# A sixth key step of each group summed by GpSimd for the softmax denominators of a 16-head cross attention, TensorE left with one

## The chip, the cores and the metric

One core of one Trainium2 chip runs the kernel. The metric is device time in microseconds (us) of one launch; less is better. Time before: 4722.19 us, the median of 3 runs (4709.07 to 4722.22).

## The reference, cut to what matters

The program runs four layers, each an attention block and a feed-forward block with a residual, on x (8 batches of 256 tokens, 128 wide) and a context (8 batches of 1601 tokens, 64 wide). The change is in the second attention of layer 1 only: 16 heads of 32, queries from x, keys and values from the normalized context.

```
H, D, C1, C2, S, M, B, W = (16, 32, 128, 64, 256, 64, 2, 4)
q = jnp.einsum('bsc,hcd->bhsd', xn, wq)
k = jnp.einsum('btc,hcd->bhtd', yn, wk)
v = jnp.einsum('btc,hcd->bhtd', yn, wv)
a = jax.nn.softmax(jnp.einsum('bhsd,bhtd->bhst', q, k) * D ** (-0.5), axis=-1)
o = jnp.einsum('bhst,bhtd->bhsd', a, v)
o = o.transpose(0, 2, 1, 3).reshape(x.shape[0], x.shape[1], H * D)
x_out = x + o @ li1_w + li1_b
```

The sum over the keys that softmax divides by (the denominator) is what the change is about.

## The kernel before, in words

The function `wide_cross` computes this attention. The work is cut into 32 groups (`NG`): 8 batches by 4 groups of 4 heads, a head on 32 partitions. The 1601 keys of a group are 13 tiles of up to 128 keys, taken two at a time in 7 key steps w = 0 to 6 (`NW`); the last step has one tile of 65 keys.

The order of the work is written out by hand: `wide_plan` repeats one list, `period`, for every n, and each engine walks through the same plan and does those steps that are its own, strictly in that order. An entry ("scores", 0, w) belongs to group n, ("max", 1, i) to group n+1, ("sums", -1) to group n-1. The steps are:

- "max": TensorE multiplies queries by keys (line 1800) into a ring of three PSUM banks, and VectorE takes the row maxima from there (line 1904). The ring is used by one such step at a time: the matmuls of the next wait until VectorE has read it. The eleventh step ends with VectorE's small reduction to the negated maximum `negm` (line 1909).
- "cut": after the eleventh "max" step of a group GpSimd splits `negm` into two bf16 pieces, `max_pieces` (a cast, line 1960, and a subtraction, line 1962). It stands in GpSimd's queue behind the additions of the group before.
- "neg": TensorE transposes the pieces (line 1810) into the ring, VectorE copies them out as `max_rows` (line 1917).
- "scores": TensorE puts the negated maxima (line 1773) and queries by keys (line 1778) for one key step into the four score banks; ScalarE takes the exponential into one of four buffers `probs` (line 1879, two instructions; line 1884 for the last step). `NPR` is 4, so the exponential of a key step waits for whoever still reads the buffer of four key steps earlier.
- "weigh": TensorE multiplies `probs` by the values (line 1821).
- the denominators: GpSimd copies the `probs` of w = 0 to `sums` (line 1949) and adds those of w = 1 to `NADD`-1 to it (line 1952), each as soon as ScalarE has written it. TensorE then multiplies a matrix of ones by `sums` (line 1829) and, for the key steps from `NADD` on, by `probs` itself (line 1834).
- "take": VectorE inverts the denominators (line 1925) and scales the output (line 1927). The next group's "weigh" of w = 0 waits for it.
- "kproj", "vproj", "qproj": projections of keys (line 1788, two groups ahead), values (line 1760, one ahead) and, for n = 2, 6, 10, ..., queries (line 1749); "out" (line 1844) for n = 4, 8, ... is the output projection.

The end of the period, the seam to the next group, reads:

```
("scores", 0, 6), ("max", 1, 9), ("kproj", 2),
("max", 1, 10), ("weigh", 0, 5), ("max", 2, 0), ("vproj", 1), ("neg", 1), ("weigh", 0, 6), ("max", 2, 1)]
```

and its start `("scores", 0, 0), ("max", 1, 2), ("sums", -1), ("qproj", 2), ("take", -1), ("max", 1, 3), ("scores", 0, 1)`. The waits that the prediction speaks of are these, in TensorE's "neg" and "sums" and in GpSimd's part:

```
pe.wait_ge(cut, 2 * n + 2)
pe.wait_ge(added, NADD * n + NADD)
for w in range(NADD, NW):
if kind == "scores" and step[2] < NADD:
    pool.wait_ge(added, NADD * n + w)
elif kind == "max" and step[2] == 10:
    pool.wait_ge(placed, n + 1)
```

Of the kernel before, what the change touches and what calls it, by code (L numbers as in the profile page):

```python
# [1635 lines left out]


NW = 7
NADD = 5
NPR = 4  # L1640


# [35 lines left out]
def wide_cross(nc, k, scale, ctx_t, xt, wq, wk, wv, w1, b1, x, xo):  # L1678
    plan, slot, ring = wide_plan()
    with ExitStack() as ctx:  # L1680
# [29 lines left out]
        def wait_drained(eng, step):  # L1710
            eng.wait_ge(s_free, slot[step] + 1)
# [15 lines left out]
        def rows(j):  # L1727
            return slice(32 * j, 32 * j + 32)
# [13 lines left out]
        def _(pe):  # L1742
            for step in plan:
# [80 lines left out]
                elif kind == "sums":  # L1824
                    n = step[1]
                    pe.wait_ge(added, NADD * n + NADD)
                    for i in range(2):
                        for j in range(4):
                            pe.matmul(lbank[rows(j), :], ones_f[:], acc[:, n % 2, j, i, :], start=(i == 0), stop=False)
                    for w in range(NADD, NW):  # L1830
                        wait_drained(pe, ("scores", n, w))
# [17 lines left out]
        def _(act):  # L1849
            for step in plan:  # L1850
# [15 lines left out]
                elif kind == "scores":  # L1866
                    n, w = step[1], step[2]
                    u = NW * n + w
                    if u >= NPR:
                        m, before = (u - NPR) // NW, (u - NPR) % NW  # L1870
                        act.wait_ge(pv_done, u - NPR + 1)
                        if before < NADD:
                            act.wait_ge(added, NADD * m + before + 1)
                        else:
# [61 lines left out]
        def _(pool):  # L1936
# [4 lines left out]
            for step in plan:  # L1941
                kind = step[0]
                if kind == "scores" and step[2] < NADD:
                    n, w = step[1], step[2]
# [5 lines left out]
                    else:  # L1950
                        pool.wait_ge(added, NADD * n + w)
                        pool.tensor_tensor(o, o, p, ALU.add).then_inc(added, 1)  # L1952
# [633 lines left out]
```

## Time and profile before

| | |
|---|---|
| median of 3 runs | 4722.19 us |
| the profiled execution | 4737.31 us |
| its span | 4735.6 us |
| TensorE busy | 3735.6 us (79%) |
| VectorE busy | 2568.1 us (54%) |
| ScalarE busy | 1959.9 us (41%) |
| GpSimd busy | 935.6 us (20%) |
| the stage of this attention | about 2117 to 3262 us of the span |

The profile comes from one execution on the chip. PE is TensorE's matmuls, PEld its weight loads, DVE is VectorE, ACT ScalarE, POOL GpSimd. Busy time is the time in which an engine had an instruction running; it says nothing of which engine the others wait for. PEclk is the clock that TensorE was granted, 1.00 being 2.4 GHz and 0.50 being 1.2 GHz.

### The profile page before, as it was taken

Reading aid. Unit: us, or ns where it says so; the run is one execution under the profiler, and the core shown is the slowest. Engines: PE = TensorE matmul, PEld = TensorE weight load, DVE = VectorE, ACT = ScalarE, POOL = GpSimd, SP = SyncE. Lnnn points to the kernel's source line nnn. Section 1 sums busy time; section 2 is a strip of 40 time slices with the busy share of each in tenths; the row PEclk is TensorE's granted clock in tenths of the full one; section 3 lists DMA queues with packets and bytes.
Section 4 is the critical chain, followed back from the end, with each engine's and each line's share of the span. In section 5 each row is a group of like instructions: output and inputs, shape, how many; then the busy total and the mean of one; then the engine's idle time right before and its main releaser. Section 6 shows DMA issues by size and latency. Waiting matters only on the chain. (4 is left out here: it accounts for less than half of the span.)

```text
span 4735.6 us, 83741 instructions
## 1 busy us (share of the span) xinstructions
PE 3735.6 (79%) x32681; PEld 1978.3 (42%) x32681; DVE 2568.1 (54%) x4933; ACT 1959.9 (41%) x2627; POOL 935.6 (20%) x546
## 2 busy tenths in 40 slices
PE   6887699999559999628999999997587669999932
PEld 4665233332336666413444444444355323333312
DVE  3434587877254455244555555552242557788856
ACT  2333376777123333223444444443121136677721
POOL 0000111110000000023656565563000011111000
PEclk9998699999579999858999999998787768999966
DMA  0000312110000000030000000000021031111000
GB/s 15 0 0 19 64 29 45 31 36 10 2 12 0 0 0 0 7 78 1 9 8 9 9 8 6 4 2 8 10 53 35 21 63 28 37 37 36 13 5 9
DMA packets 68487, 89.57 MB, mean 19 GB/s; under 512 B 37808, under 2 KB 48718, under 8 KB 68174
## 3 DMA queue, kind: packets, MB, share of 16 engines
q1 hardware_dynamic: 59416, 75.78, 7.2%
q10 hardware_dynamic: 8758, 9.41, 0.9%
q8 instruction: 220, 3.60, 0.3%
q14 instruction: 93, 0.76, 0.1%
HBM read 34.53 MB, written 4.33 MB: 8 GB/s over the span
## 5 line engine op out<-in xcount | busy, mean ns | idle before, releaser
L1592 DVE TENSOR_REDUCE mx<-ps 128x2 f32<-128x802 f32 (+1 forms) x1372 | 1028.0, 778 | 295.0 <-PE ps L1458 271.5
L1526 ACT ACTIVATE probs<-ps 128x1024 f32<-128x1024 f32 (+1 forms) x832 | 832.9, 1024 | 256.0 <-PE ps L1444 247.1
L1904 DVE TENSOR_REDUCE mx<-ps 128x3 f32<-128x1203 f32 (+1 forms) x352 | 483.2, 1373 | 476.2 <-PE ps L1800 476.2
L1952 POOL TENSOR_TENSOR sums<-sums,probs 128x2048 f32<-128x2048 f32 x128 | 579.0, 4523 | 142.5 <-ACT probs L1879 128.8
L1458 PE MATMUL ps<-kt,qs 48*128 48x401 bf16 x2048 | 472.8, 356 | 112.1 <-DVE mx L1592 75.3
L1476 PE MATMUL ps<-probs,v_cur 128*9 128x256 f32 x6656 | 530.7, 392 | 0.4 <-ACT probs L1526 0.4
L1879 ACT ACTIVATE probs<-ps 128x1024 f32<-128x1024 f32 x384 | 372.1, 1021 | 358.2 <-PE ps L1778 358.1
L1800 PE MATMUL ps<-kt,qt 32*128 32x401 f32 x2048 | 338.3, 554 | 47.1 <-DVE mx L1904 41.5
L1444 PE MATMUL ps<-qs,kt 50*128 50x256 bf16 (+1 forms) x3328 | 347.6, 282 | 1.8 <-ACT probs L1526 1.4
L462 PE MATMUL ps<-kk,q 128*128 128x256 f32 (+1 forms) x1024 | 277.2, 390 | 25.2 <-ACT kk L541 20.8
L1458 PEld LDWEIGHTS ps<-kt,qs 48*128 48x128 bf16 x2048 | 134.9, 95 | 328.7 <-DVE mx L1592 251.4
L539 ACT ACTIVATE q<-ps,qb 32x256 f32<-32x256 f32 (+1 forms) x256 | 119.5, 467 | 348.1 <-PE ps L455 344.0
L1778 PE MATMUL ps<-qt,kt 32*128 32x256 f32 (+1 forms) x3328 | 251.1, 375 | 0.0
L1444 PEld LDWEIGHTS ps<-qs,kt 50*128 50x128 bf16 (+1 forms) x3328 | 111.3, 97 | 327.8 <-issue 153.5
L547 ACT ACTIVATE probs<-ps 128x384 f32<-128x384 f32 (+1 forms) x256 | 137.9, 542 | 259.4 <-PE ps L483 135.2
L1821 PE MATMUL ps<-probs,v_cur 128*32 128x256 f32 (+1 forms) x3328 | 227.0, 387 | 12.9 <-issue 12.7
L1633 POOL CAST max_pieces<-negm 128x8 bf16<-128x8 f32 x64 | 12.1, 189 | 1120.9 <-DVE negm L1597 1120.9
L462 PEld LDWEIGHTS ps<-kk,q 128*128 128x128 f32 x1024 | 184.0, 202 | 68.4 <-ACT kk L541 32.1
L1800 PEld LDWEIGHTS ps<-kt,qt 32*128 32x128 f32 x2048 | 110.6, 186 | 200.5 <-DVE mx L1904 119.0
L1778 PEld LDWEIGHTS ps<-qt,kt 32*128 32x128 f32 (+1 forms) x3328 | 188.0, 180 | 12.0
L568 DVE TENSOR_REDUCE mpad<-ps 128x2 f32<-128x512 f32 x128 | 88.7, 693 | 185.5 <-PE ps L462 183.5
L168 PE MATMUL ps<-ident,xn 128*128 128x128 f32 x160 | 41.4, 430 | 179.4 <-DVE xn L154 179.4
(382 smaller groups left out, 5243.7 us busy)
## 6 DMA issues: line engine op xcount, KB each, us to landing
kt<-k SPq DMA_DIRECT2D x776, 50.0 KB
ctx_s<-in_ctx_t SPq DMA_DIRECT2D x16, 400.2 KB, 4.8
ctx_s<-ctx_norm_t SPq DMA_DIRECT2D x16, 400.2 KB, 5.4
qs<-q ACTq DMA_DIRECT2D x24, 192.0 KB
ctx_norm_t<-ctx_norm_t SPq DMA_DIRECT2D x8, 400.2 KB, 3.7
ctx_a<-in_ctx_t SPq DMA_DIRECT2D x8, 400.2 KB, 4.3
ctx_b<-in_ctx_t SPq DMA_DIRECT2D x8, 400.2 KB
ctx_tok<-in_ctx SPq DMA_DIRECT2D x8, 384.0 KB
```

The lines of the kernel that those rows point to most:

```text
L462: ins = pe.matmul(ring(step)[:, S * qt:S * qt + nk], q1[:, g, j, P * qt:P * qt + P], kk[:, g, 0:nk], start=True, stop=True)
L1444: ins = pe.matmul(pair[0:m, j, S * (jj // 2):S * (jj // 2) + S], kt[rows, b % 2, g, P * t:P * t + m], qs[rows, g, S * b:S * b + S], start= ...
L1458: ins = pe.matmul(bank(step, i)[:, 0:CH], qs[rows, g, tok:tok + P], kt[rows, b % 2, g, lo:lo + CH], start=True, stop=True)
L1476: ins = pe.matmul(obank[32 * jj:32 * jj + 9, :], v[0:m, b % 2, t, 9 * h:9 * h + 9], pr[0:m, u % 3, at:at + S], start=(t == 0), stop=(t == ...
L1526: act.activation(pr[0:m, u % 3, :], pair[0:m].rearrange("p a n -> p (a n)"), ACT.Exp, scale=scale).then_inc(s_free, 1)
L1592: dve.tensor_reduce(mx[:, n % 2, i0:i0 + count], src, AX_X, ALU.max).then_inc(freed(step), 1)
L1778: ins = pe.matmul(sbanks[0:m, j, S * i:S * i + S], kt[rows(j), n % 4, P * t:P * t + m], qt[rows(j), b % 2, a, :], start=False, stop=(i == ...
L1800: ins = pe.matmul(rbanks[:, i - 3 * i0, 0:CH], qt[rows(j), b % 2, a, q:q + P], kt[rows(j), n % 4, lo:lo + CH], start=True, stop=True)
L1821: ins = pe.matmul(obank[rows(j), :], v[0:m, n % 2, t, rows(j)], pr[0:m, (NW * n + w) % NPR, j, i, :], start=(t == 0), stop=(t == KT - 1))
L1879: ins = act.activation(pr[:, u % NPR, 2 * f:2 * f + 2, :, :].rearrange("p j i n -> p (j i n)"), sbanks[:, 2 * f:2 * f + 2, :].rearrange("p ...
L1904: dve.tensor_reduce(mx[:, n % 2, 3 * i0:3 * i0 + count], rbanks[:, 0:count, 0:CH], AX_X, ALU.max).then_inc(ring_free, 1)
L1952: pool.tensor_tensor(o, o, p, ALU.add).then_inc(added, 1)
```

## The change

The constant `NADD` goes from 5 to 6. No other line changes.

```diff
 NW = 7
-NADD = 5
+NADD = 6
 NPR = 4
```

On GpSimd, the seam between two groups: `sums` are the running denominators, `max_pieces` the split maxima of the next group. Before:

```order
226 L1960 CAST max_pieces<-negm 128x8
227 L1962 TENSOR_TENSOR max_pieces<-negm,max_pieces 128x8
228 L1949 COPY sums<-probs 128x2048
229 L1952 TENSOR_TENSOR sums<-sums,probs 128x2048 x4
230 L1960 CAST max_pieces<-negm 128x8
231 L1962 TENSOR_TENSOR max_pieces<-negm,max_pieces 128x8
```

And with the change:

```order
226 L1960 CAST max_pieces<-negm 128x8
227 L1962 TENSOR_TENSOR max_pieces<-negm,max_pieces 128x8
228 L1949 COPY sums<-probs 128x2048
229 L1952 TENSOR_TENSOR sums<-sums,probs 128x2048 x5
230 L1960 CAST max_pieces<-negm 128x8
231 L1962 TENSOR_TENSOR max_pieces<-negm,max_pieces 128x8
```

A fifth addition stands ahead of the cast and the subtraction of every group.

On TensorE, the start of a group: the scores of w = 0, a "max" step, the denominators of the group before (lines 1829 and 1834), the next "max" step and the scores of w = 1:

```order
@@ -2046,5 +2046,5 @@
 L1800 MATMUL ps<-kt,qt 128x401 x3
 L1829 MATMUL ps<-sums,ones_f 32x256 x8
-L1834 MATMUL ps<-probs,ones_f 32x256 x12
+L1834 MATMUL ps<-probs,ones_f 32x256 x4
 L1800 MATMUL ps<-kt,qt 128x401 x3
 L1773 MATMUL ps<-max_rows,ones_b 128x512 x4
```

Eight of twelve matmuls on `probs` are gone; the order of the rest is the same. The instructions of VectorE and ScalarE are the same ones in the same order.

## Rows read from the trace of the kernel before

**Rows 1.** Busy time of each engine over the stage of this attention.

```profile
core 0: us, PE busy (x) PEld busy (x) DVE busy (x) ACT busy (x) POOL busy (x), PEclk, DMA share, GB/s
2117.00:3262.00 1145.00, 1024.57 (x12236) 535.73 (x12236) 569.28 (x486) 515.87 (x553) 654.55 (x227) 0.98 0.03 7
```

**Rows 2.** Groups of GpSimd's instructions by line, in the stage.

```profile
L1952 POOL TENSOR_TENSOR sums<-sums,probs 128x2048 f32<-128x2048 f32 x128 | 579.0, 4523 | 142.5 <-ACT probs L1879 128.8
```

**Rows 3.** Timeline, GpSimd, four groups on end: start, duration, engine, line, [idle before].

```profile
2587.25 18.55 POOL L1952 TENSOR_TENSOR sums<-sums,probs 128x2048 f32<-128x2048 f32 x4 [3.55 <-ACT probs L1879]
2610.03 0.22 POOL L1960 CAST max_pieces<-negm 128x8 bf16<-128x8 f32 x1 [4.24 <-DVE negm L1909]
...
2623.20 18.51 POOL L1952 TENSOR_TENSOR sums<-sums,probs 128x2048 f32<-128x2048 f32 x4 [3.56 <-ACT probs L1879]
2643.21 0.22 POOL L1960 CAST max_pieces<-negm 128x8 bf16<-128x8 f32 x1 [1.50 <-DVE negm L1909]
2643.51 0.23 POOL L1962 TENSOR_TENSOR max_pieces<-negm,max_pieces 128x8 bf16<-128x8 f32 x1
...
2658.79 18.54 POOL L1952 TENSOR_TENSOR sums<-sums,probs 128x2048 f32<-128x2048 f32 x4 [5.97 <-ACT probs L1879]
2678.37 0.22 POOL L1960 CAST max_pieces<-negm 128x8 bf16<-128x8 f32 x1 [1.04 <-DVE negm L1909]
...
2691.54 18.53 POOL L1952 TENSOR_TENSOR sums<-sums,probs 128x2048 f32<-128x2048 f32 x4 [3.55 <-ACT probs L1879]
2711.53 0.22 POOL L1960 CAST max_pieces<-negm 128x8 bf16<-128x8 f32 x1 [1.46 <-DVE negm L1909]
```

**Rows 4.** Timeline, the seam after the group whose additions began at 2623.20.

```profile
2643.93 1.82 PE L1760 MATMUL ps<-wv,ctx_s 64*128 64x128 f32 x26
2645.68 0.29 PE L1810 MATMUL ps<-identb,max_pieces 128*128 128x128 bf16 x2
...
2646.47 0.95 PE L1800 MATMUL ps<-kt,qt 32*128 32x401 f32 x6
2647.51 0.10 PEld L1773 LDWEIGHTS ps<-max_rows,ones_b 2*128 2x128 bf16 x4 [0.74 <-ACT v_cur L1865]
2647.54 1.41 DVE L1904 TENSOR_REDUCE mx<-ps 128x3 f32<-128x1203 f32 x1 [1.18 <-PE ps L1800]
2649.01 0.95 PE L1800 MATMUL ps<-kt,qt 32*128 32x401 f32 x6 [0.24 <-DVE mx L1904]
```

**Rows 5.** Timeline, the denominators at the start of a group.

```profile
2616.90 1.41 DVE L1904 TENSOR_REDUCE mx<-ps 128x3 f32<-128x1203 f32 x1 [1.13 <-PE ps L1800]
2617.60 1.48 PE L1834 MATMUL ps<-probs,ones_f 128*32 128x256 f32 x24
2619.01 0.61 PE L1800 MATMUL ps<-kt,qt 32*128 32x401 f32 x3
2621.18 1.94 ACT L1879 ACTIVATE probs<-ps 128x1024 f32<-128x1024 f32 x2 [3.49 <-PE ps L1778]
```

**Rows 6.** The instructions of line 1834: duration of one pass in ns, min/median/max.

```profile
L1834 PE MATMUL ps<-probs,ones_f x768: 377/379/634, 2205.1 to 3259.9; 128*32 128x256 f32 x128, 65*32 65x256 f32 x64
```

**Rows 7.** Timeline, the last group's denominators.

```profile
3256.34 1.93 PE L1829 MATMUL ps<-sums,ones_f 128*32 128x256 f32 x16 [2.23 <-POOL sums L1952]
3258.04 2.28 PE L1834 MATMUL ps<-probs,ones_f 128*32 128x256 f32 x24
```

**Rows 8.** Timeline of TensorE near the stage's end.

```profile
3223.79 0.94 PE L1800 MATMUL ps<-kt,qt 32*128 32x401 f32 x4 [1.61 <-DVE mx L1904]
...
3225.73 3.35 PE L1760 MATMUL ps<-wv,ctx_s 64*128 64x128 f32 x26
...
3244.68 0.39 PE L1773 MATMUL ps<-max_rows,ones_b 2*128 2x512 bf16 x4 [1.15 <-ACT probs L1879]
```

**Rows 9.** Windows there, columns as in rows 1.

```profile
3224.00:3228.00 4.00, 4.00 (x40) 2.78 (x40) 1.20 (x2) 0.00 (x0) 1.73 (x3) 0.69 0.00 0
3244.00:3248.00 4.00, 2.26 (x36) 1.22 (x36) 0.00 (x0) 2.53 (x3) 3.86 (x2) 1.00 0.00 0
```

## The prediction

> **What bounds the kernel now.** I first took the busy times over the stage [rows 1]. It lasts 1145 us. TensorE is busy 1025 of them, GpSimd 655, VectorE 569, ScalarE 516. Read alone, that says: TensorE is full, GpSimd has 490 us to spare, so work should go from the one to the other. Busy time does not say who waits for whom at the place where the work is put, so I went on to the timelines.
>
> GpSimd's timeline [rows 3] shows one pattern per group. Four additions run end to end, 18.5 us in all, from the moment the exponential of w = 1 is done; call that moment S. GpSimd is never idle between them. A short wait for `negm` follows, and then the cast. That wait is the real slack of GpSimd here: 1.50, 1.04 and 1.46 us in three groups of four, 4.24 us in the one that holds the output projection. The idle time that makes up the rest of the 490 us lies elsewhere, ahead of the copy and between the copy and the first addition, where the new addition can't go, since w = 5 is not computed yet.
>
> The seam [rows 4] shows who needs the cast. TensorE runs the values' projection, the transposes of the pieces right at its end, then a "max" step at 2646.47, whose read by VectorE ends at 2648.95, and the next "max" step at 2649.01, 0.06 us later. The ring is handed over without slack: a transpose that comes late makes both steps late, then the denominators behind them, the scores of w = 1, and the next S.
>
> **The change, part by part.** Every group repeats; I work per group and multiply.
>
> *The addition.* One addition takes 4.52 us [rows 2]; four take 18.53, so they start every (18.53 - 4.52) / 3 = 4.67 us [rows 3]. Five end at S + 4 x 4.67 + 4.52 = S + 23.2. The w = 5 data should be there: GpSimd ran through w = 1 to 4 without idle time, so each of them was ready before it came to it, and w = 5 has until S + 18.6, 4.67 us longer than w = 4, whereas its two exponentials take 1.94 us [rows 5]. The cast can begin at S + 23.3.
>
> *How late that is.* Before, the casts began at S + 22.78, 20.01, 19.58 and 19.99 for the four kinds of group [rows 3]. So they move by 0.5, 3.3, 3.7 and 3.3 us.
>
> *What hides a part of it.* From the cast's start to the transposes it was 2645.68 - 2643.21 = 2.47 us [rows 3, 4]. What has to lie there is the cast and the subtraction, 0.53 us in all (2643.21 to 2643.74), and the step from GpSimd to TensorE. The hand-overs in the rows take 0.06 us, for instance VectorE's read that ends 2648.95 and TensorE's step at 2649.01 [rows 4]; I take that for GpSimd too, whose own hand-over to TensorE at the stage's end [rows 7] is of the same kind. So 2.47 - 0.59 = 1.9 us of lateness cost nothing; the values' projection covers them. What is left is 0, 1.4, 1.8 and 1.4 us. If the cover did not exist it would be the whole 3.3 to 3.7; if the later wait for ScalarE's values copy (0.74 us of TensorE's idle time, at 2647.51 [rows 4]) hid more, it would be 0.7 to 1.1. I take 1.4 and 1.8, since the "max" steps of the ring don't wait for that copy and they are the longer way.
>
> Of the 31 seams 24 are of the late kinds: 8 of 1.8 (a query projection in the group) and 16 of 1.4. 8 x 1.8 + 16 x 1.4 = 36.8 us.
>
> *The eight matmuls taken away.* Twelve matmuls are 24 passes and take 1.48 us, of which the last pass's own 0.38 us [rows 6] is not shortened: (1.48 - 0.38) / 23 x 16 = 0.77 us less [rows 5]. The "max" step behind them begins 2619.01 and would begin 18.24, but VectorE frees the ring at 2618.31 [rows 5]; so 0.64 us are won, and 0.77 where the query projection stands between. This is on the path: ScalarE waits 3.49 us for the scores of w = 1 behind it [rows 5]. Bounds: nothing, if something else held w = 1, and 0.77 in all. 30 groups have it inside the stage: 23 x 0.64 + 7 x 0.77 = 20.1 us won.
>
> *The stage's end.* After the last group TensorE already waits 2.23 us for GpSimd [rows 7]; one more addition is 4.67 us on the path, and the eight matmuls less, at the half clock there, give back (2.28 - 0.63) / 23 x 16 = 1.15 [rows 6, 7]. Net 3.5 us.
>
> Sum so far: 36.8 + 3.5 - 20.1 = +20 us.
>
> *The clock.* The steady stage has no pause of TensorE as long as the new ones. Near its end it has two kinds [rows 8, 9]: pauses of 1.15 us in every key step leave the granted clock at 1.00 (3244 to 3248), and one of 1.61 us, at 3222.18 to 3223.79, is followed by 0.69 in 3224 to 3228. The clock fell to its lower level, 1.2 GHz, and the values' projection took 3.35 us there, against 1.82 at 2.4 GHz [rows 4, 8]. The new pauses, between the projection and the transposes, are as long as the lateness: 1.4 us lies between the pause that was harmless and the one that was not, 1.8 us a little above both. The 24 seams all have one. The longest cost that I see for a fall is those 1.5 us; the least is nothing, when the slow stretch lies where TensorE waits for ScalarE or GpSimd anyway. Behind the seam TensorE's steps are on the path, so I take 1.2. With half of the seams it is 12 x 1.2 = +14 us; with none 0, with all and 1.5 each +36.
>
> In the Trainium skill, the page "TensorE: Matmul & The Clock Gate", section "Why this matters for your kernels", warns only of pauses longer than any that this change makes. By that rule no seam would lose the clock and the sum would stop at +20. The 1.61 us pause in this trace speaks against relying on it.
>
> **Sum: +20 + 14 = +34 us.** Against its own execution that is 4737.31 + 34 = 4771 us. That execution is 15 us (0.3%) above the median of the runs shown; against the median it is 4722.2 + 34 = 4756 us, +0.7%. A difference under 0.3%, 14 us, can't be told from none.
>
> **The rivals.**
>
> *The clock never falls* (chance 0.22). For it: pauses of 1.15 us never cost it. Against: the 1.61. Time: +20 us, 4742.
>
> *It falls at every seam, at full price* (0.10). +20 + 36 = +56, 4778. For it: the one pause of 1.61 us was followed by a fall. Against: 16 of the new pauses are shorter than that one.
>
> *The values copy covers more* (0.12). If the scores of w = 0 and not the ring led to the next S, the lateness would shrink by the 0.74 us of that wait at each seam: 36.8 - 24 x 0.74 = 19.0, and 19.0 + 3.5 - 20.1 = +2: 4724, no change. Against it: VectorE's hand-over of the ring at 2649.01 with no slack.
>
> *Faster* (0.06). One mechanism: the seam can absorb all of the late cast. It would take a path from the seam to S that has 1.4 to 1.8 us more slack than the rows show, for instance if TensorE took the shortened denominators and the "max" steps before the transposes; the plan has them behind. Then only the eight matmuls and the end count: 3.5 - 20.1 = -17 us, 4705. It decides at a lateness of 0.7 us per seam (20.1 - 3.5, over 24); I work out twice that.
>
> *The fifth case, mine: some seams lose the clock* (0.50).
>
> That the change would not do what it says is excluded: the order of instructions has the fifth addition ahead of each cast and four matmuls in the place of twelve.
>
> **How the numbers follow.** The likeliest case is +34: 4756. From +14 (the first rival, less the small noise of a median) to +60 the clock cases lie, 0.82 together; leaving out the two lower rivals would be 0.18. So the range is 4736 to 4782. Slower by over 0.3%: the case itself 0.50, all seams 0.10, and most of the 0.22, together 0.79. Within 0.3%: 0.12 and the rest of the 0.22, 0.15. Faster: 0.06.
>
> **What would show it.** GpSimd: five additions in 23.2 us, then the cast with hardly any idle time ahead of it, in all groups. TensorE: a wait for GpSimd's `max_pieces` of 1.4 or 1.8 us ahead of line 1810 in three groups of four, none in the fourth. Line 1834: 8 passes per group instead of 24, about 0.7 us. Four groups together grow by 1.9 us where the clock holds: lateness 1.4 + 1.8 + 1.4 = 4.6, less 3 x 0.64 + 0.77 = 2.7. The granted clock: stretches at 0.50 behind seams in a steady part that had none. The prediction is wrong if the wait ahead of line 1810 is under 0.7 us, if S does not follow the transposes one for one, or if the granted clock stays at 1.00 (then about 4742) or falls behind all seams (about 4778).

## The result and the profile after

| | before | after |
|---|---|---|
| median | 4719.67 us (4 runs) | 4751.32 us (4 runs, 4749.49 to 4759.3) |
| profiled execution | 4737.31 us | 4759.3 us |
| span | 4735.6 us | 4757.5 us |

The ratio is 1.0075, 95% interval 1.0055 to 1.0094: the kernel is 0.75% slower. 4756 us were forecast.

The stage of the cross attention, which answers to [rows 1], from the view of windows (columns as there):

```profile
2117.00:3285.00 1168.00, 1017.29 (x11700) 536.25 (x11700) 567.63 (x485) 516.00 (x553) 791.10 (x258) 0.95 0.03 8
2200.00:3200.00 1000.00, 891.60 (x10420) 476.23 (x10416) 506.68 (x436) 454.60 (x488) 704.06 (x228) 0.97 0.03 6
```

The steady 1000 us of the kernel before, to compare with the second of these rows:

```profile
2200.00:3200.00 1000.00, 916.92 (x11144) 482.26 (x11142) 518.38 (x444) 468.40 (x503) 592.53 (x203) 1.00 0.03 6
```

TensorE has fewer instructions and GpSimd more, as wanted. But the granted clock, which was 1.00 in this part before, is now 0.97.

GpSimd's timeline for two groups, which answers to [rows 3]:

```profile
2780.74 23.19 POOL L1952 TENSOR_TENSOR sums<-sums,probs 128x2048 f32<-128x2048 f32 x5 [2.92 <-ACT probs L1879]
2803.89 0.21 POOL L1960 CAST max_pieces<-negm 128x8 bf16<-128x8 f32 x1
...
2816.72 23.19 POOL L1952 TENSOR_TENSOR sums<-sums,probs 128x2048 f32<-128x2048 f32 x5 [5.37 <-ACT probs L1879]
2839.85 0.22 POOL L1960 CAST max_pieces<-negm 128x8 bf16<-128x8 f32 x1
2840.15 0.23 POOL L1962 TENSOR_TENSOR max_pieces<-negm,max_pieces 128x8 bf16<-128x8 f32 x1
```

The rows of the cast have no bracket any more: GpSimd does not wait for the maxima, the maxima wait for GpSimd. In the late kinds of group the cast begins 23.12 to 23.15 us after S (S is the start of the first addition), where it was 19.4 to 20.3 before.

The seam behind the second of these groups, as the timeline shows it, answers to [rows 4]:

```profile
2837.02 1.82 PE L1760 MATMUL ps<-wv,ctx_s 64*128 64x128 f32 x26
...
2840.44 0.29 PE L1810 MATMUL ps<-identb,max_pieces 128*128 128x128 bf16 x2 [1.60 <-POOL max_pieces L1962]
...
2842.50 1.93 PE L1778 MATMUL ps<-qt,kt 32*128 32x256 f32 x14
2843.88 1.73 PE L1800 MATMUL ps<-kt,qt 32*128 32x401 f32 x6
```

TensorE stands 1.60 us before the transposes, and GpSimd's subtraction is what ends the wait. The scores and the "max" step behind it are then slow: six passes of line 1800 take 1.73 us and not the 0.95 of [rows 4]. That is the lower clock, in a window of the same place (columns as above):

```profile
2841.00:2846.00 5.00, 5.00 (x49) 3.08 (x45) 1.81 (x3) 1.41 (x2) 0.00 (x0) 0.66 0.56 131
```

How often TensorE waits there is in the view of line 1810, what ended the idle time ahead of it (us, times). Each seam counts twice, for the matmul and for its weight load, so these are 24 seams. TensorE's own pause is 1.1 to 1.8 us in 23 of them and 3.21 us in the last:

```profile
  POOL max_pieces L1962: 79.9, 48
```

And the end of the stage, in the timeline, answers to [rows 7]:

```profile
3291.80 1.94 PE L1829 MATMUL ps<-sums,ones_f 128*32 128x256 f32 x16 [6.88 <-POOL sums L1952]
3293.51 1.08 PE L1834 MATMUL ps<-probs,ones_f 65*32 65x256 f32 x8
```

The wait for GpSimd's last addition is 6.88 us, 4.65 longer.

**A measure for the experiments.** The stage can be cut out of each trace: from the first S to the last S (31 group lengths), and from the last S to the end of VectorE's last read of the output projection. In the trace before the additions start at 2177.52 and 3237.76, and that read ends at 3268.44. After:

```profile
2181.24 4.53 POOL L1952 TENSOR_TENSOR sums<-sums,probs 128x2048 f32<-128x2048 f32 x1 [4.06 <-ACT probs L1879]
...
3268.59 4.52 POOL L1952 TENSOR_TENSOR sums<-sums,probs 128x2048 f32<-128x2048 f32 x1 [2.03 <-ACT probs L1879]
```

So the groups took 1060.24 us before and 1087.35 after (+27.1), the end 30.7 and 34.4 (+3.7). What lies behind the stage is the same code in every kernel here, yet took 1467 us in the trace before and 1449 to 1459 in the others. That is why single spans say less than the stage, and why the whole launches are compared by medians. Each stage time comes from one execution of its kernel; how well such times repeat shows where two kernels do the same: 29 of the 31 groups of e1_cut_first below are as long as those of e3_matmuls_only within 0.01 us.

### The profile page after: what moved, and what is told of

Same layout as the page of the kernel before. It is cut to its first block and busy times, and to the rows that moved or that the text cites. A ratio compares the mean times of both kernels' runs of the same rounds, so it can differ in the third digit from the quotient of the medians.

```text
span 4757.5 us, 82781 instructions
## 1 busy us (share of the span) xinstructions
PE 3719.5 (78%) x32169; PEld 1974.9 (42%) x32169; DVE 2567.6 (54%) x4933; ACT 1960.9 (41%) x2627; POOL 1079.3 (23%) x578
## 5 line engine op out<-in xcount | busy, mean ns | idle before, releaser
L1952 POOL TENSOR_TENSOR sums<-sums,probs 128x2048 f32<-128x2048 f32 x160 | 723.7, 4523 | 131.0 <-ACT probs L1879 112.3
L1800 PE MATMUL ps<-kt,qt 32*128 32x401 f32 x2048 | 353.5, 572 | 49.4 <-DVE mx L1904 42.2
L1778 PE MATMUL ps<-qt,kt 32*128 32x256 f32 (+1 forms) x3328 | 277.3, 394 | 0.0
L1778 PEld LDWEIGHTS ps<-qt,kt 32*128 32x128 f32 (+1 forms) x3328 | 204.0, 190 | 14.1
```

The source lines that it names most:

```text
L1778: ins = pe.matmul(sbanks[0:m, j, S * i:S * i + S], kt[rows(j), n % 4, P * t:P * t + m], qt[rows(j), b % 2, a, :], start=False, stop=(i == ...
L1800: ins = pe.matmul(rbanks[:, i - 3 * i0, 0:CH], qt[rows(j), b % 2, a, q:q + P], kt[rows(j), n % 4, lo:lo + CH], start=True, stop=True)
```

## The experiments

| run | median us | before beside it | ratio (95% interval) | first to last S | end | falls of the clock between them |
|---|---|---|---|---|---|---|
| kernel before | | | | 1060.2 | 30.7 | 1 |
| kernel after | 4751.3 | 4719.7 | 1.0075 (1.0055 to 1.0094) | 1087.3 | 34.4 | 15 |
| e1_cut_first | 4708.3 | 4719.4 | 0.9983 (0.9966 to 1.0) | 1032.1 | 34.4 | 0 |
| e2_add_only | 4772.1 | 4719.4 | 1.0111 (1.0092 to 1.013) | 1104.4 | 36.1 | 10 |
| e3_matmuls_only | 4692.5 | 4719.4 | 0.9939 (0.9921 to 0.9957) | 1035.9 | 29.4 | 1 |
| e4_fill | 4743.1 | 4719.4 | 1.0046 (1.003 to 1.0061) | 1071.3 | 34.4 | 1 |
| e5_four_steps | 4739.9 | 4721.0 | 1.004 (1.0027 to 1.0053) | 1084.6 | 26.7 | 0 |
| e6_half_add | 4696.7 | 4721.0 | 0.9947 (0.9929 to 0.9964) | 1035.8 | 32.2 | 1 |
| e7_cut_first_short_end | 4688.3 | 4721.0 | 0.9936 (0.9919 to 0.9953) | 1033.5 | 27.0 | 1 |

The theory: the cost is the cast, which stands behind the fifth addition in GpSimd's queue; TensorE's seam waits for it, and the pauses lower the clock. The rivals: GpSimd's additions slow the others by running at all; or the matmuls taken away gained nothing.

**e1_cut_first.** GpSimd's part of the changed kernel, with the cast and the subtraction ahead of the addition of w = 5:

```diff
-            for step in plan:
+            order = [s for s in plan if s[0] == "scores" and s[2] < NADD or s[0] == "max" and s[2] == 10]
+            for i in range(len(order) - 1):
+                if order[i][0] == "scores" and order[i][2] == NADD - 1 and order[i + 1][0] == "max":
+                    order[i], order[i + 1] = order[i + 1], order[i]
+            for step in order:
```

> The changed kernel, but GpSimd splits the next group's maxima (cast and subtraction) before its addition of w = 5 instead of after it; nothing else differs. Late-cut theory (the cost of the change is the cast that stands behind the fifth addition): the casts are back at S + 19.6 to 20.3 us and S + 22.8 us, TensorE no longer waits ahead of line 1810, the granted clock stays at 1.00 in the steady part, and what is left is the eight matmuls less (20 us won) and the longer end of the stage (3.5 us lost): -17 us against the kernel before, about 4703, ratio 0.9965. Rival A (GpSimd's addition itself slows the others, by sharing memory or ports with VectorE and ScalarE): the order does not matter, about 4750 remains. Rival B (the denominators wait for the sixth addition): as the addition now ends only at about S + 25 us, TensorE would wait ahead of line 1829, and the time stays above the kernel before.

Measured: 0.9983, with an interval of 0.9966 to 1.0, so the 0.9965 forecast is just outside and the gain in the whole launch (11 us by the medians, where 17 were forecast) is barely clear of none. In the stage it is clear: 1032.1 us to the last S, 28.1 less than before and 55.2 less than after. GpSimd's timeline in this run:

```profile
2774.62 18.54 POOL L1956 TENSOR_TENSOR sums<-sums,probs 128x2048 f32<-128x2048 f32 x4 [5.11 <-ACT probs L1879]
2794.20 0.22 POOL L1964 CAST max_pieces<-negm 128x8 bf16<-128x8 f32 x1 [1.04 <-DVE negm L1909]
2794.49 0.23 POOL L1966 TENSOR_TENSOR max_pieces<-negm,max_pieces 128x8 bf16<-128x8 f32 x1
2794.66 4.52 POOL L1956 TENSOR_TENSOR sums<-sums,probs 128x2048 f32<-128x2048 f32 x1
2801.92 1.89 POOL L1953 COPY sums<-probs 128x2048 f32<-128x2048 f32 x1 [2.75 <-ACT probs L1879]
```

The cast waits for VectorE again, the fifth addition fills idle time that was there, and 2.75 us are still idle behind it. All five additions are done in every group, as in the changed kernel, and yet 29 of the 31 groups are as long, within 0.01 us, as in e3_matmuls_only, where GpSimd has four. So the rival of a general slowing by GpSimd falls. Ahead of the denominators TensorE waits for an addition only at the last seam (0.67 us, where the keys' projection and most "max" steps are gone from the plan) and at the stage's end, so rival B falls too. Windows of this run:

```profile
2200.00:3200.00 1000.00, 913.95 (x10962) 474.19 (x10958) 529.53 (x454) 479.75 (x515) 745.51 (x240) 1.00 0.03 6
```

**e2_add_only.** GpSimd as changed, TensorE still multiplying w = 5 too (`w` from `NADD - 1` on); w = 5 is counted twice, and ScalarE waits for both readers before it overwrites that buffer.

```diff
-                    for w in range(NADD, NW):
+                    for w in range(NADD - 1, NW):
...
-                        else:
+                        if before >= NADD - 1:
```

> The changed kernel, but TensorE still runs the matmuls of w = 5 as well (twelve, not four), so w = 5 is counted twice in the denominators; GpSimd as in the changed kernel. Late-cut theory: the pauses ahead of line 1810 stay as in the changed kernel (1.4 and 1.6 us in three groups of four), the 20 us of the matmuls are not won, the last group's end costs 4.7 instead of 3.5: +35 for the seams, +5 for the end, +14 for clock falls, +54 us against the kernel before, about 4774, ratio 1.0115. Rival (the matmuls taken away won nothing, something else held the scores of w = 1): no slower than the changed kernel, about 4751.

Measured: 1.0111 against 1.0115 forecast. The addition alone costs 44 us to the last S and 5.4 at the end. From the transposes to the next S it is 10.69 us in this run where the clock holds, 10.06 in the changed kernel: the matmuls do count. The clock fell 10 times and not 15. The pauses are 1.2 us in most of the 16 seams in which the changed kernel has 1.4: the cast comes 23.1 us after S in both, but TensorE reaches the seam 0.23 us later with the longer denominators, as the next run explains. These shorter pauses are followed by a fall more rarely, but not never. One that is, with the window behind it:

```profile
2738.36 0.28 PE L1810 MATMUL ps<-identb,max_pieces 128*128 128x128 bf16 x2 [1.19 <-POOL max_pieces L1962]
...
2740.50:2747.40 6.90, 6.89 (x60) 2.71 (x52) 2.54 (x2) 1.94 (x2) 1.89 (x1) 0.51 0.01 2
```

**e3_matmuls_only.** The kernel before, with TensorE leaving out w = 5; nobody adds it.

```diff
-                    for w in range(NADD, NW):
+                    for w in range(NADD + 1, NW):
```

> The kernel before, but TensorE leaves out the matmuls of w = 5 (four, not twelve), and nobody adds w = 5, so the denominators lack it; GpSimd as before. It measures the gain alone. Theory: 0.64 us in 23 groups, 0.77 in 7, 1.15 at the end: -21 us, about 4699, ratio 0.9955, and the time from the transposes to the next S is 10.06 us where it was 10.69. Rival (no gain, since scores of w = 1 wait for something else): within 5 us of the kernel before.

Measured: 0.9939, more than forecast (0.9955); to the last S 24.4 us won where 20.1 were forecast, and 1.3 at the end. The timeline shows why:

```profile
2606.46 18.52 POOL L1952 TENSOR_TENSOR sums<-sums,probs 128x2048 f32<-128x2048 f32 x4 [2.92 <-ACT probs L1879]
2626.24 0.22 POOL L1960 CAST max_pieces<-negm 128x8 bf16<-128x8 f32 x1 [1.25 <-DVE negm L1909]
2633.96 1.89 POOL L1949 COPY sums<-probs 128x2048 f32<-128x2048 f32 x1 [7.19 <-ACT probs L1879]
```

In three of four kinds of group the cast comes 0.23 us sooner after S than in [rows 3] (19.78 for 20.01 here): the 0.64 us won at w = 1 have become 0.87 by the seam. ScalarE's rows of w = 1 and w = 2 in a group of this run show where the rest comes from. Its wait for the scores of w = 2 is 1.65 us, and 1.87 in the kernel before; the "max" step that TensorE has ahead of those scores begins 0.62 us before S here (2672.45) and 0.39 us before S there (2691.15, S at 2691.54):

```profile
2671.06 1.94 ACT L1879 ACTIVATE probs<-ps 128x1024 f32<-128x1024 f32 x2 [2.86 <-PE ps L1778]
2674.64 1.94 ACT L1879 ACTIVATE probs<-ps 128x1024 f32<-128x1024 f32 x2 [1.65 <-PE ps L1778]
```

In the changed kernel the cast hangs on GpSimd, and this part turns into a longer pause. The gain is larger still if the last group is left out: the first 30 groups are 25.5 us shorter than before, the last one is 1.1 us longer, since more of it ran at the lower clock.

**e4_fill.** The changed kernel, with three unused matmuls in the pause of 23 of the 24 late seams; the first seam has none:

```diff
-                    pe.wait_ge(cut, 2 * n + 2)
                     wait(pe, ring_free, ring[step])
+                    if n >= 1 and n % 4 != 1:
+                        for i in range(FILL):
+                            pe.matmul(rbanks[:, 1, 0:S], k.ident[:], xt[:, 0:S], start=True, stop=True)
+                    pe.wait_ge(cut, 2 * n + 2)
```

> The changed kernel, but in the three late kinds of seam TensorE runs three 128x256 f32 matmuls (about 1.3 us, their result unused) into a free bank of the ring while it would wait for the cast. The pause is filled, nothing else moves. Clock theory (15 falls of the granted clock in the changed kernel's steady stage cost about 14 us together): the clock stays at 1.00 in the steady part, the times from transposes to the next S are all 10.06 or 12.25 us, and the kernel is 12 to 15 us faster than the changed one, about 4737, ratio 1.0037. Rival (the falls cost nothing, because slow stretches lie where TensorE waits anyway): same time as the changed kernel, 4751, or a little more if the filling matmuls come out longer than the pause.

Measured: 1.0046, forecast 1.0037; the ratio is 0.0029 below the changed kernel's, 14 us. The two intervals just overlap, so the stage has to carry this: to the last S it is 16.1 us shorter. The seam and the window:

```profile
2836.39 1.56 PE L1811 MATMUL ps<-xt,ident 128*128 128x256 f32 x6
2838.07 0.28 PE L1814 MATMUL ps<-identb,max_pieces 128*128 128x128 bf16 x2
...
2200.00:3200.00 1000.00, 913.00 (x10681) 489.29 (x10684) 513.66 (x440) 462.59 (x497) 716.45 (x232) 1.00 0.03 6
```

The transposes are as late as in the changed kernel (23.72 us after S), but TensorE is busy until then and the clock stays at 1.00. From the transposes to the next S it is 10.06 us, where the changed kernel has 10.94 behind most falls. So 16 us of the loss are the clock. The one fall that is left follows the pause of 1.90 us in the first seam, the one without these matmuls. Read seam by seam, the 14 falls of the changed kernel that the kernel before did not have cost 15.1 us between the transposes and the next S, which agrees.

**e5_four_steps.** `NADD` = 4, the other way:

```diff
-NADD = 6
+NADD = 4
```

> The change the other way: GpSimd takes four key steps (three additions), TensorE three. Late-cut theory, in which GpSimd's additions count only where the cast stands behind them: the casts, which waited for the maxima already with five steps, do not come earlier relative to the transposes, no pause of TensorE appears, and eight matmuls more cost 0.64 to 0.87 us per group: +24 us, less about 3 at the end of the stage, where GpSimd is done sooner: +21 against the kernel before, about 4741, ratio 1.0045. Rival (each addition costs the other engines something wherever it stands): one addition less wins back what the sixth cost, and the kernel is not slower than before.

Measured: 1.004, forecast 1.0045; +24.3 us to the last S (forecast +24), -3.9 at the end (forecast -3). GpSimd's row:

```profile
2598.57 13.86 POOL L1952 TENSOR_TENSOR sums<-sums,probs 128x2048 f32<-128x2048 f32 x3 [4.41 <-ACT probs L1879]
2621.34 0.22 POOL L1960 CAST max_pieces<-negm 128x8 bf16<-128x8 f32 x1 [8.92 <-DVE negm L1909]
```

It waits 8.92 us for the maxima in the group with the output projection, and nobody gains by it: in all groups but the first and the last the cast and the transposes keep their places after S within 0.01 us, and 29 of the 31 groups grow by 0.85 or 0.86 us, which the eight matmuls more account for (eight matmuls less win 0.85 us a group in the mean of the first 30 of e3_matmuls_only). Where the cast was not late, an addition less gains nothing.

**e6_half_add.** The changed kernel, with the addition of w = 5 over half of the heads; the other half's denominators lack w = 5.

```diff
+                        if w == 5:
+                            o, p = o[:, 0:2, :, :], p[:, 0:2, :, :]
                         pool.tensor_tensor(o, o, p, ALU.add).then_inc(added, 1)
```

> The changed kernel, but the addition of w = 5 takes only two of the four heads, half the elements (2.3 us instead of 4.5); the other two heads' denominators lack w = 5. Late-cut theory with 1.9 us of cover: casts at S + 21.0 us, 1.0 to 1.5 us late and under the cover, so no pause ahead of line 1810, no fall of the clock, and the stage up to the last S is as short as with the matmuls alone taken away (1036 us, against 1087 with the full addition): about -23 us against the kernel before, 4697, ratio 0.995. Rival (the lateness counts in full, without cover): half the loss remains, the stage up to the last S at about 1060.

Measured: 0.9947, forecast 0.995, and 1035.8 us to the last S, what e3_matmuls_only has without a fifth addition (1035.9).

```profile
2608.48 21.02 POOL L1954 TENSOR_TENSOR sums<-sums,probs 128x2048 f32<-128x2048 f32 x5 [2.92 <-ACT probs L1879]
2629.45 0.22 POOL L1962 CAST max_pieces<-negm 128x8 bf16<-128x8 f32 x1
```

The cast is late here too (no wait ahead of it, S + 20.97 us), but by no more than 1.4 us, and the cover hides it whole. How far the cover reaches is read from the full addition: in the group of e4_fill whose additions begin at 2814.33 the cast is 3.56 us later than in e3_matmuls_only (S + 23.14 for 19.58), the transposes 1.67 us, and the group is 1.67 us longer. So the cost is a threshold, not a slope: about 1.9 us of lateness are free, what is beyond counts in full.

**e7_cut_first_short_end.** e1_cut_first, with GpSimd taking four key steps in the last group alone (beside the lines of e1_cut_first, where the list of GpSimd's steps is cut in the same way; `LAST` is 4):

```diff
-                    pe.wait_ge(added, NADD * n + NADD)
+                    pe.wait_ge(added, NADD * n + (LAST if n == NG - 1 else NADD))
...
-                    for w in range(NADD, NW):
+                    for w in range(LAST if n == NG - 1 else NADD, NW):
```

> GpSimd splits the maxima before its addition of w = 5, as in the run with that order, and in the last group alone it takes four key steps instead of six, TensorE three, since nothing follows there that could hide the additions. Theory: up to the last S as in that run (1032 us), and from there to the stage's end about 28 us instead of 34.4, since TensorE no longer waits 6.9 us for the last addition: -27 us against the kernel before, about 4693, ratio 0.9943. Rival (the end is bound by ScalarE's exponentials or by the slow clock, not by the additions): no more than 2 us won there.

Measured: 0.9936 (0.9919 to 0.9953), forecast 0.9943: faster than both kernels, 33 us below the one before. The end takes 27.0 us (28 forecast). Its timeline:

```profile
3219.45 0.64 PE L1822 MATMUL ps<-probs,v_cur 65*32 65x256 f32 x8 [0.23 <-ACT probs L1885]
3219.91 1.05 PE L1830 MATMUL ps<-sums,ones_f 128*32 128x256 f32 x16
3220.77 2.35 PE L1835 MATMUL ps<-probs,ones_f 128*32 128x256 f32 x40
```

TensorE goes from the last "weigh" straight to the denominators, at full clock, and its 40 passes take 2.35 us, about as long as 24 did at the lower clock after the wait (2.28 [rows 7]).

## Why the prediction was right, point by point

- *The addition.* Five end at S + 23.2 and the cast follows at S + 23.14, forecast S + 23.3. It starts with no gap behind the last addition, where I had allowed 0.1 us.
- *The lateness.* Pauses of mostly 1.4 and 1.6 us, forecast 1.4 and 1.8, in 24 seams and none in the fourth kind. The casts came 0.17 us sooner than forecast, which shortens the pauses; the 0.23 us by which TensorE reaches the seam sooner (e3_matmuls_only) lengthen those of 1.4 again. Sum: from e3_matmuls_only to e4_fill, which has the late casts without the falls, 35.4 us; forecast 36.8. That up to 1.4 us of lateness cost nothing is shown by e6_half_add, and that the cover is 1.9 us by e4_fill against e3_matmuls_only.
- *That the ring and not the values copy leads to the next S.* From the transposes to the next S it is 10.06 us with late and with timely transposes alike (e4_fill, e1_cut_first). The rival by which the copy covers more falls with it.
- *The matmuls.* -20.1 forecast, -24.4 measured by themselves (e3_matmuls_only); the term was too small by the 0.23 us of the scores of w = 2 in most groups, and by 0.1 us where the query projection stands between; the last group, 1.1 us longer, hides a part of this. So four groups together grow by 1.2 us where the clock holds (137.45 us before, 138.64 in e4_fill), where 1.9 were forecast.
- *The end.* +3.5 forecast, +3.7 measured.
- *The clock.* 14 falls more than before, forecast 12; together 16.1 us (from e4_fill to the changed kernel), forecast 14. One costs 0.9 us in most cases and about 2.3 in two, where I took 1.2 for all. This was the step that I chose rather than read: half of the seams, from a single pause of 1.61 us, and a price between the bounds. That there are such falls in some of the seams and not in all was right; that the product came within 2 us is in part luck.
- *The sum.* In the stage: -24.4 + 35.4 + 16.1 + 3.7 = +30.8 us; the medians differ by 31.7; forecast +34. The largest error of a term is the 4.3 us of the matmuls; the excess of the falls (2.1) made up for half of it.
- *The faster rival* was wrong for this kernel, but names what e1_cut_first does: a seam that does not feel the addition.

What stays open: e1_cut_first won 28 us up to the last S, but its median is only 11 us below the one before, while e7_cut_first_short_end with the same order won 33 us. The runs of e1_cut_first spread from 4693 to 4732 us, and the code outside the stage, the same in all, is where such differences lie in the traces; what makes them was not tried. The record shows this much: five of its twelve launches had a mean granted clock of 0.883 to 0.886 and took 4711 to 4732 us, the other seven had 0.889 to 0.894 and took 4693 to 4711, with a median of 4697; none of the 19 launches of the kernel before beside it, and none of e7_cut_first_short_end, was below 0.887. The trace is from one of the seven, so that this order keeps the clock in the stage is shown for such a launch alone.

## What to carry to other kernels

Before work goes to an engine with idle time, look at what stands behind the place in its queue: GpSimd had 490 us to spare in this stage, but only 1.0 to 1.5 us ahead of the one short instruction that the others wait for. With the same five additions and the same matmuls the 31 groups took 27 us longer than before where that instruction stood behind them, and 28 us less where it went ahead of the last one. And where a stall is added, count the clock too: here 16 of the some 51 us lost at the seams were not the waiting but the slow matmuls behind it.

## What the runs showed of the hardware

Pauses of TensorE of 1.15 to 1.82 us can be followed by a fall of its granted clock. In the changed kernel's trace 8 of 9 pauses of 1.59 us or more ahead of the transposes were followed by a fall to 0.50 that the kernel before did not have, and 6 of the 14 of 1.1 to 1.6 us. In e2_add_only it was 5 of the 7 of 1.59 us or more and 3 of the 16 of 0.9 to 1.3 us, the shortest of them 1.15 us. Yet the pauses of 1.15 us in each key step at the stage's end were not followed by one [rows 8, 9], nor was the pause of 1.61 us in e1_cut_first (3190.17 to 3191.78) at the place of the one that was in [rows 8]. So the length of the pause alone does not decide it; what else does was not tried. The Trainium skill ("TensorE: Matmul & The Clock Gate", section "Why this matters for your kernels") warns of longer ones only, such as the 3.21 us at the last seam; the measurement decides. Three unused matmuls in the pause (1.56 us busy) kept the clock at 1.00 and were worth 16 us in the stage.

An addition of 128x2048 f32 on GpSimd takes 4.52 us in the changed kernel as in [rows 2], with 32 more of them. VectorE's read of three banks takes 1.41 us with an addition beside it (at 2837.21 in the changed kernel) and without one (at 2842.42). The page "GPSIMD Engine Reference" of the Trainium skill, section "3.1 Elementwise — side-by-side cycle accounting", gives 4497 ns for that addition; the trace agrees.
